# Packed first loads on two queues, a reordered first batch and a reordered end of the last batch in a two-layer MLP with expert output columns

## The reference, cut to what matters

```
h        = gelu(x @ W1 + b1)                    # W1: 512 x 2048
shared   = h @ W2 + b2                          # W2: 2048 x 384
expert_b = h_b @ We[idx_b] + be[idx_b]          # We: 8 x 2048 x 128, one expert for each batch
out      = x + concatenate([shared, expert], -1)
```

## Time and profile before

| what | value |
|---|---|
| median of 3 runs | 1210.66 us (1210.32 to 1212.32) |
| the profiled execution: its own time | 1210.57 us |
| the profiled execution: its span | 1208.8 us |
| TensorE (PE) busy | 1200.3 us, 99% of the span |
| VectorE (DVE) busy | 1063.3 us, 88% |
| ScalarE (ACT) busy | 767.9 us, 64% |
| DMA, mean over the span | 72 GB/s |
| mean granted TensorE clock | 0.999 of full |

### The profile page before, as it was taken

One profiled execution on the slowest core, in us unless ns is written; L12 is line 12 of the kernel. 1 busy time (PEld: TensorE's weight loads), 2 busy tenths in 40 slices (PEclk: granted clock), 3 DMA queues, 4 the chain that ended last, 5 costly groups with the idle time before them and its releaser, 6 DMA issues.

```text
span 1208.8 us, 26221 instructions
## 1 busy us (share of the span) xinstructions
PE 1200.3 (99%) x10284; PEld 1007.5 (83%) x10284; DVE 1063.3 (88%) x1399; ACT 767.9 (64%) x1027; POOL 4.6 (0%) x12
## 2 busy tenths in 40 slices
PE   9999999999999999999999999999999999999998
PEld 4456667778888888888888888888888888888887
DVE  6998888788989988899988989889899888999886
ACT  3765556576766667566765756767666675667652
POOL 0000000000000000000000000000000000000000
PEclk9999999999999999999999999999999999999999
DMA  7316522112131121211212021120311212012101
GB/s 278 105 70 231 198 95 71 36 36 71 36 105 36 35 70 49 91 35 35 71 68 69 35 72 67 35 69 35 104 35 35 69 48 90 35 35 71 70 36 36
DMA packets 38813, 86.61 MB, mean 72 GB/s; under 512 B 5872, under 2 KB 6128, under 8 KB 36208
## 3 DMA queue, kind: packets, MB, share of 16 engines
q1 hardware_dynamic: 37616, 77.63, 19.0%
q0 software_dynamic: 1152, 8.39, 1.9%
HBM read 69.22 MB, written 16.78 MB: 71 GB/s over the span
## 4 chain that ended last, share of the span: by engine, by line
PE 93%; DVE 5%; issue 1%; ACT 1%; DMA 0%; SPq 0%; ACTq 0%; DVEq 0%
PE banks L1635 15%; PE banks L1637 15%; PE banks L1636 15%; PE q_ps L1635 9%; PE q_ps L1637 9%; PE q_ps L1636 9%; PE out_ps L1636 7%; PE out_ps L1635 7%; PE out_ps L1637 7%; DVE h_ring L946 1%; DVE w_max L932 1%; DMA h_ring<-w1f_dram 0%; DVE x_lo L946 0%; ACT u L758 0%; DVE w_lo L946 0%
## 5 line engine op out<-in xcount | busy, mean ns | idle before, releaser
L1635 PE MATMUL banks<-x_hi,w_hi 128*128 128x256 f16 (+1 forms) x1704 | 467.0, 274 | 0.2 <-ACT kept L726 0.2
L1636 PE MATMUL banks<-x_lo,w_hi 128*128 128x256 f16 (+1 forms) x1704 | 467.0, 274 | 0.0
L1637 PE MATMUL banks<-x_hi,w_lo 128*128 128x256 f16 (+1 forms) x1704 | 467.0, 274 | 0.0
L946 DVE SCALAR_TENSOR_TENSOR h_ring<-u,scale,h_ring 128x1536 f16<-128x1536 f32 (+2 forms) x121 | 253.8, 2099 | 24.3 <-ACT h_ring L606 20.4
L726 ACT ACTIVATE kept<-banks 128x512 f32<-128x512 f32 x180 | 106.2, 590 | 173.6 <-PE banks L1637 173.6
L1635 PEld LDWEIGHTS banks<-x_hi,w_hi 128*128 128x128 f16 x1704 | 166.7, 98 | 29.0 <-ACT kept L726 1.0
L1636 PEld LDWEIGHTS banks<-x_lo,w_hi 128*128 128x128 f16 x1704 | 166.7, 98 | 27.2 <-issue 0.3
L1637 PEld LDWEIGHTS banks<-x_hi,w_lo 128*128 128x128 f16 x1704 | 166.7, 98 | 22.0
L758 ACT ACTIVATE u<-u,b_sb,undo 128x512 f32<-128x512 f32 x120 | 91.1, 806 | 101.3 <-DVE u L1254 101.3
L1637 PE MATMUL q_ps<-h_ring,w_lo 128*128 128x256 f16 (+1 forms) x504 | 144.2, 286 | 0.0
L1635 PE MATMUL q_ps<-h_ring,w_hi 128*128 128x256 f16 (+1 forms) x504 | 144.2, 286 | 0.0
(11 more groups left out here) (186 smaller groups left out, 2076.5 us busy)
## 6 DMA issues: line engine op xcount, KB each, us to landing
out_dram<-x_raw SPq DMA_DIRECT2D x63, 256.0 KB, 2.4
x_raw<-x_dram SPq DMA_DIRECT2D x60, 256.0 KB, 4.1
t_sum<-w2o_dram SPq DMA_DIRECT2D x26, 512.0 KB, 3.8
t_sum<-we_dram SPq DMA_DIRECT2D x26, 512.0 KB, 4.3
w_sums<-we_dram POOLq DMA_DIRECT2D x8, 1024.0 KB, 6.5
h_ring<-w_dram SPq DMA_DIRECT2D x5, 1024.0 KB, 8.9
e_raw<-we_dram SPq DMA_DIRECT2D x3, 1024.0 KB, 4.7
t_sum<-w2p_dram SPq DMA_DIRECT2D x2, 1024.0 KB, 4.8
```

Source lines behind the costliest of these rows:

```text
L946: return nc.vector.scalar_tensor_tensor(to, of, s, hi, ALU.mult, ALU.subtract)
L1635: nc.tensor.matmul(ps, hi, v_hi, start=start, stop=False, skip_group_check=True)
L1636: nc.tensor.matmul(ps, hi, v_lo, start=False, stop=False, skip_group_check=True)
L1637: return nc.tensor.matmul(ps, lo, v_hi, start=False, stop=stop, skip_group_check=True)
```

## The change

- The first loads are packed: a new array `first` of two halves, each 128 partitions by 8 KB. Half 0 holds x's input tiles 0 and 1 and W1's (group 0) input tiles 0 and 1, half 1 the rest. Half 0 is loaded by two queues, partitions 0 to 63 by SP and 64 to 127 by ScalarE's (ACT's) queue, half 1 by SP. They land in the ring `h_ring`, no longer in `x_raw`; x of batch 0 is loaded once more into `x_raw[:, 0]` behind W2 of group 2, for the residual. 26 warm-up matmuls become 22.
- TensorE's sum for the scale of x stands behind the fifth matmul of `first_group` instead of behind the third, that for W1's group 1 behind the tenth instead of the ninth, and the other sums of W1, of W2 and of the expert's weights stand later; for batch 0 `e_total` is now behind the sixth unit of layer 2, for batches 1 and 2 behind P2 of step (b, 1).
- VectorE and ScalarE do the work of the first batch in another order. W1's group 1 has its maximum ahead of the lo parts of x; W1's group 2 gets its scale ahead of the maximum of group 0; `w1_split(3)` stands ahead of `h_split(0, 0)`; `w2_split(0)` stands ahead of `e_top(0)`, `w2_split(1)` ahead of `e_scales`, and ScalarE's last two gelus of batch 0 ahead of the expert's splits.
- W2's load of group 3 also waits for the lo parts of x.
- In `TAIL` P1 and P2 of tiles 2 and 3 come ahead of those of tiles 0 and 1, VectorE takes the former first, and the last store of tile 3 is issued by ScalarE.

```
-WARM = 26
+WARM = 22
-TAIL = ((0, P1, 0), (0, P2, 0), (1, P1, 0), (1, P2, 0), (1, P4, 0), (1, P5, 0), (0, P6, 0), (0, P5, 0),
+TAIL = ((1, P1, 0), (1, P2, 0), (0, P1, 0), (0, P2, 0), (1, P4, 0), (1, P5, 0), (0, P6, 0), (0, P5, 0),
...
+        first_raw = h_ring[:, :, :, :, :].rearrange("p r s a n -> p (r s a n)").bitcast(F32)[:, KC * N:3 * KC * N]
+        def first_x_raw(k):
+            return first_raw[:, (k if k < KH else KC + k) * N:][:, :N]
...
-            half = 2 * BLOCK
-            for k in range(2):
-                sp.dma_start(x_raw[:, 0, KH * k:KH * (k + 1)], x[0, :, KH * k:KH * (k + 1)]
-                             ).then_inc(first_x_loaded[k], 16)
-                sp.dma_start(w1_raw(0)[:, half * k:half * (k + 1)], w1f[:, half * k:half * (k + 1)]
-                             ).then_inc(w1_rest_loaded if k else w1_loaded[0], 16)
+            sp.dma_start(first_raw[:P // 2, :KC * N], first[0, :P // 2]).then_inc(first_loaded[0], 16)
+            sp.dma_start(first_raw[:, KC * N:], first[1]).then_inc(first_loaded[1], 16)
...
+            sp.dma_start(x_raw[:, 0], x[0]).then_inc(first_x_again, 16)
+
             sp.wait_ge(w1_max_done, D)
             sp.wait_ge(first_l1_done, C)
+            sp.wait_ge(first_x_lo, KC)
             load_w2(3)
...
-            for o in (1, 2, 3):
+            for o in (1, 2):
                 store(B - 1, 1, o)
...
+            nc.scalar.dma_start(first_raw[P // 2:, :KC * N], first[0, P // 2:]).then_inc(first_loaded[0], 16)
             act.wait_ge(ones_set, 1)
...
             w1_split(2)
-            h_split(0, 0, 0)
             first_gelu(1, 1)
             first_gelu(1, 2)
+            first_gelu(1, 3)
             w1_split(3)
-            first_gelu(1, 3)
+            h_split(0, 0, 0)
             h_split(0, 0, 1)
...
             first_gelu(3, 1)
+            first_gelu(3, 2)
+            first_gelu(3, 3)
             e_split(0, 0)
             e_split(0, 1)
-            first_gelu(3, 2)
-            first_gelu(3, 3)
...
+            act.wait_ge(out_ready[3], B)
+            nc.scalar.dma_start(out[B - 1, 3], x_raw[:, 1, 3]).then_inc(out_stored[3], 16)
...
             first_x_scale()
+            w1_top(1)
             first_x_split(0)
             first_x_split(1)
-            w1_top(1)
             first_x_split(2)
+            w1_scales(1, 3)
             first_x_split(3)
-            w1_scales(1, 3)
+            w1_split(1, 0, 2)
             w1_top(2)
-            w1_split(1, 0, 2)
             w1_split(1, 2, 2)
             w1_top(3)
+            w1_scales(2, 5)
             w1_top(0)
             first_h_top()
-            w1_scales(2, 7)
+            w1_split(2)
             w1_scales(3, 9)
             first_h_scale()
             w1_scales(0, 13)
-            w1_split(2)
+            w1_split(3)
             h_split(0, 0, 0)
-            w1_split(3)
             for d in range(D):
                 w2_top(d)
             h_split(0, 1, 0)
             w2_scales()
+            w2_split(0)
             e_top(0)
-            w2_split(0)
+            w2_split(1)
             e_scales(0, 0)
             e_split(0, 0)
-            w2_split(1)
             e_split(0, 1)
...
-            mix(B - 1, 1, 0)
             take_c11(B - 1, 1)
             take_p1(B - 1, 1, True)
+            mix(B - 1, 1, 0)
             take_xy(B - 1, 1, False)
...
-                        pe.wait_ge(first_x_loaded[k // KH], 16)
-                        pe.wait_ge(w1_loaded[0] if k == 0 else w1_rest_loaded, 16)
+                        pe.wait_ge(first_loaded[k // KH], 16 if k > 0 else 32)
...
-                        if k == 0 and c == 2:
+                        if k == 1 and c == 0:
                             pe.wait_ge(first_x_max_done, KC)
                             total(first_x_tops, first_x_max[:, :]).then_inc(first_x_all_done, 1)
-                        if k == KH and c == 0:
+                        if k == KH and c == 1:
                             w1_total(1)
...
-                    if c == 1:
+                    if c == 0:
+                        w1_total(2)
+                    if c == 3:
 
                         x_total(0)
-                        for d in (2, 3, 0):
+                        for d in (3, 0):
                             w1_total(d)
...
-                    if c == 0:
+                    if c == 1:
                         pe.wait_ge(w2_max_done, D)
...
-                    if c == 2:
-                        e_total(0)
                 for unit in range(OT * C):
                     layer2(0, 0, unit)
+                    if unit == C + 1:
+                        e_total(0)
```

More of the change, by code:

```diff
@@ L86, with build @@
 TOP_SUMS, TOP = 12, 14
-def build(nc, x, idx, w1, w1f, w2, w2p, w2o, we, b1, b2, be, out):
+def build(nc, x, idx, w1, first, w2, w2p, w2o, we, b1, b2, be, out):
     with ExitStack() as ctx:
@@ L166, in build @@
         x_loaded = [sem("x_loaded_even"), sem("x_loaded_odd")]
-        first_x_loaded = [sem(f"first_x_loaded{k}") for k in range(2)]
-        w1_loaded = [sem(f"w1_loaded{d}") for d in range(D)]
-        w1_rest_loaded = sem("w1_rest_loaded")
+        first_loaded = [sem(f"first_loaded{k}") for k in range(2)]
+        first_x_again = sem("first_x_again")
+        w1_loaded = [None] + [sem(f"w1_loaded{d}") for d in range(1, D)]
         w1_reloaded = sem("w1_reloaded")
@@ L266, in place @@
             return h_ring[:, r, part].rearrange("p a n -> p (a n)").bitcast(F32)
+        first_raw = h_ring[:, :, :, :, :].rearrange("p r s a n -> p (r s a n)").bitcast(F32)[:, KC * N:3 * KC * N]
+        def first_x_raw(k):
+            return first_raw[:, (k if k < KH else KC + k) * N:][:, :N]
         def w1_raw(d):
+            if d == 0:
+                return first_raw[:, KH * N:(KH + KC) * N]
             if d == 2:
@@ L273, in w1_raw @@
                 return t_sum[:, :, :, :].rearrange("p a k n -> p (a k n)")
-            return place(d, 1)
+            return place(1, 1)
         s_sum = place(1, 1)
@@ L554, in first_x_split @@
                 act.wait_ge(x_scaled, 1)
-                nc.scalar.activation(first_x[0][:, k], x_raw[:, 0, k], ACT.Copy,
+                nc.scalar.activation(first_x[0][:, k], first_x_raw(k), ACT.Copy,
                                      scale=scale[:, 0, 0:1]).then_inc(first_x_hi, 1)
@@ L701, in residual @@
                 if isinstance(b, int) and b == 0:
-                    act.wait_ge(first_x_lo, KC)
+                    act.wait_ge(first_x_again, 16)
                     act.wait_ge(b2_loaded, 16)
@@ L948, in first_x_top @@
             def first_x_top(k):
-                dve.wait_ge(first_x_loaded[k // KH], 16)
-                top(first_x_max[:, k:k + 1], x_raw[:, 0, k]).then_inc(first_x_max_done, 1)
+                dve.wait_ge(first_loaded[k // KH], 16 if k >= KH else 32)
+                top(first_x_max[:, k:k + 1], first_x_raw(k)).then_inc(first_x_max_done, 1)
             def h_top(b):
@@ L967, in w1_top @@
             def w1_top(d):
-                dve.wait_ge(w1_loaded[d], 16)
                 if d == 0:
-                    dve.wait_ge(w1_rest_loaded, 16)
+                    dve.wait_ge(first_loaded[0], 32)
+                    dve.wait_ge(first_loaded[1], 16)
+                else:
+                    dve.wait_ge(w1_loaded[d], 16)
                 top(w_max[:, d:d + 1], w1_raw(d)).then_inc(w1_max_done, 1)
@@ L1026, in w1_scales @@
             def w1_scales(d, base):
-                dve.wait_ge(w1_all_done, 1 if d == 1 else D)
+                dve.wait_ge(w1_all_done, d if d in (1, 2) else D)
                 power(w1_tops[:, d:d + 1], w_exps[:, :], w1_inv[:, d:d + 1], w1_scale[:, d:d + 1], TOP_SUMS,
@@ L1033, in first_h_top @@
             def first_h_top():
-                base = 5
+                base = 7
                 dve.wait_ge(w1_max_done, D)
@@ L1062, in first_x_split @@
                 dve.wait_ge(first_x_hi, k + 1)
-                split_lo(first_x[1][:, k], x_raw[:, 0, k], scale[:, 0, 0:1], first_x[0][:, k]).then_inc(first_x_lo, 1)
+                split_lo(first_x[1][:, k], first_x_raw(k), scale[:, 0, 0:1], first_x[0][:, k]).then_inc(first_x_lo, 1)
             def add_t(b, par):
@@ L1643, in first_group @@
                     if k % KH == 0:
-                        pe.wait_ge(first_x_loaded[k // KH], 16)
-                        pe.wait_ge(w1_loaded[0] if k == 0 else w1_rest_loaded, 16)
+                        pe.wait_ge(first_loaded[k // KH], 16 if k > 0 else 32)
                     for c in range(C):
-                        last = nc.tensor.matmul(first_bank(c), raw[:, k, c], x_raw[:, 0, k],
+                        last = nc.tensor.matmul(first_bank(c), raw[:, k, c], first_x_raw(k),
                                                 start=k == 0, stop=k == KC - 1)
@@ L1882, in w1_total @@
             def w1_total(d):
-                pe.wait_ge(w1_max_done, 1 if d == 1 else D)
+                pe.wait_ge(w1_max_done, d if d in (1, 2) else D)
```

(11 more changed lines are left out.)

## The result

The changed kernel takes 1214.56 us (median of 7 runs, 1212.93 to 1216.04) against 1210.73 us before (median of 7): ratio 1.0032, 95% interval 1.0022 to 1.0042. It is slower by 3.8 us, where 1210.9 and "no difference" had been forecast. The profiled execution took 1214.53 us, its span is 1212.7 us, 3.9 us longer than before.

A forecast was written before the change was run, and what follows sets the result against it. TensorE, at 99% of the span, was taken to bound the kernel; -1.55 (landing) - 0.3 (short waits) + 2.1 (new waits) + 0 (end) = +0.3 us on 1210.57 gave 1210.9 us, range 1208.8 to 1212.5.

The forecast's parts named there:

- The landing: First packed load: half 0 lands at 5.75 (bounds 5.1 and 7.3), so TensorE starts 1.55 us earlier than 7.30.
- The slow pace of the kernel before: First loads: 248 GB/s in 2 to 4 us before; if it came again, the landing would stay at 7.3.
- The warm-ups: TensorE's start: four fewer warm-ups leave a hole under 0.7 us, the clock stays granted; cost nothing.
- The short waits: TensorE before layer 2: waits for h's scale and for W1's lo part of group 2 both go, -0.3 us.
- VectorE's lateness: First batch up to `x_top` of batch 1 (58.2): VectorE 2.8 us later while TensorE is 1.85 us earlier.
- The three waits: TensorE waits for VectorE near 75, 82 and 96: 1.5, 0.3 and 0.3 us, together +2.1 us (1.5 to 2.7).
- its first 0.3: TensorE's wait at P5 near 82, for `c11` of step (1, 0): 0.3 us.
- its second 0.3: TensorE's wait at P2 of step (1, 1) near 96, for `c12`: 0.3 us.
- The end: Tail: new order and the store moved to ScalarE's queue change nothing, 0 with 0.2 us either way.
- the cushion holds: Rival 1, VectorE's distance to TensorE: the whole head start survives, -1.85 us, 1208.7 us; chance 0.22.
- Rival 2: First load comes no earlier, pace is the bytes', TensorE starts at 7.2: +1.7 us, 1212.3; chance 0.18.
- rival 3: Second load starves ScalarE's part of half 0, TensorE starts at 8.45: +2.95 us, 1213.5; chance 0.08.

The follow-up runs named there:

- a1: Changed kernel with half 0 of the packed load issued whole by SP, 128 partitions, one queue: 1210.83 us, ratio 1.0.
- a3: Changed kernel with half 0 by two queues, each all 128 partitions and half the columns: 1210.74 us, ratio 1.0.
- a4: Changed kernel with 48 warm-up matmuls instead of 22: 1213.35 us, ratio 1.002.
- b2: Kernel before with only the new batch-0 orders of TensorE, VectorE and ScalarE, loads and tail as before: 1212.2 us, ratio 1.0014.
- b3: Kernel before with only the new tail and the last store of tile 3 by ScalarE: 1210.53 us, ratio 0.9998.
- c2: c1 with the tail of the kernel before: 1208.9 us, ratio 0.9985.
- c1: a3 with `e_top(0)` again ahead of `w2_split(0)`, `e_scales` behind it, and TensorE's `e_total(0)` ahead of layer 2: 1208.82 us, ratio 0.9986.
- a2: Changed kernel, but SP issues half 1 only when both parts of half 0 have landed: 1214.59 us, ratio 1.0031.
- b4: Changed kernel with both 64-partition parts of half 0 issued by SP, one behind the other, none by ScalarE: 1215.28 us, ratio 1.004.

## Why the prediction was wrong

**The landing** ("I take 5.75") is the step that failed. The forecast summed over bytes and bounded the pace by 8 KB rows to all 128 partitions, and took the two 64-partition parts for the same thing. For such a transfer the size was right: 5.62 in a1, 5.76 in a3. As the change writes it, half 0 is complete at 8.30, outside the bounds of 5.1 and 7.3. Against the forecast's -1.55 us the start is +1.02 us. No row of the kernel before shows a transfer to half of the partitions, so the bound on the late side should have been wider. Two of its numbers are also off in themselves: 1.8 us off 7.3 is 5.5, not 5.1, and with -0.3 and +2.1 the sum changes its sign at a landing of 5.5, not 5.4. Neither touches the result.

The slow pace of the kernel before, 248 GB/s in 2 to 4 us, is another thing, and here the forecast chose rightly. It lasts until 6 us there, and not in a1 or a3. The window from 4 to 6 us of the kernel before, to be read against the two above:

```profile
4.00:6.00 2.00, 1.80 (x14) 1.29 (x12) 0.62 (x2) 0.00 (x0) 0.00 (x0) 1.00 0.91 236
```

Packing thus does bring the data 1.5 us earlier, as long as all partitions are in each part. Why x and W1 in four separate transfers to 128 partitions each came at 236 GB/s stays open.

The Trainium skill ("DMA: Bandwidth & Descriptors", section "Issuing engines are not separate DMA queues") says that DMAs of several engines share the same 16 engines and only the issue is saved. The runs agree: with 128 partitions one queue lands at 5.62, two at 5.76; with 64, one at 8.02, two at 8.30.

Why 64 partitions halve the pace stays open. The same page, in its section "The descriptor swizzle", shows a transfer to 128 partitions with the engines 0 to 7 writing the partitions 0 to 63 and 8 to 15 the others, each engine one port of the memory. A supposition from it: if all 16 engines serve 64 partitions, two would share each port and the ports of the other 64 stand idle. That fits the full engine share at half the bytes (1.14 and 246 GB/s), and the packets, which are one part's and then the other's, so that both halves of the partitions are not written at once. But no run here counts engines or ports.

**The warm-ups** ("Nothing") failed as a consequence. The forecast leaned on a hole under 0.7 us; it became 2.96 us, the clock was granted at 0.50 in 8 to 10 us, and the float32 group took +1.34 us; the forecast put this term at nothing. a4 confirms it by taking it away. The leaning on the 1.5 us hole was also weaker than it looked: rows 2 and 4 are one execution. Of 75 executions of the kernel before that ran beside the experiments three took 1212.30 to 1212.78 us, at a mean granted clock of 0.998 against 0.999 or 1.000 in the others. The Trainium skill ("TensorE: Matmul & The Clock Gate", Part 1) states that an idle array falls back to its lower clock; these rows agree.

**The short waits** (-0.3) were worth -0.59: 2.36 us late at group 1, 1.77 at layer 2. Bracketed waits were too small a measure. From start to start of the matmuls, where the usual step is 0.22 us, the sums for h and W1 cost 0.49 us before (26.45 to 27.16) and 0.11 us in the changed kernel, and the hole ahead of group 2 cost 0.18 us (32.12 to 32.51) and nothing; the 0.49 us of the earlier trace rows are idle time of the weight loads. In a3 the same step gave -0.60 (from 1.64 to 2.24 us early).

**VectorE's lateness** was right nearly step by step: idle for ScalarE's copy 1.6 forecast, 1.64 measured; lateness against TensorE 2.8 + 1.85 = 4.65 forecast, 4.71 measured; `x_top` of batch 1 at 58.2 forecast, 57.93 in a3. The two parts of the 4.71 were less exact than their sum: in a3 VectorE is 2.48 us later and TensorE 2.24 us earlier. It is a property of the order (4.71 to 4.72 in after, a1, a3, a4 and b2), not of the loads.

**The three waits** (+2.1) measured +2.23: from 1.77 to 4.00 us late. The forecast's 1.5 us stands against 1.57 us lost up to 78.68 (a wait of 1.37 us in the row), its first 0.3 against 0.42 us up to 85.60, and its second 0.3 against 0.21 us up to 100.16, P2 of step (1, 1), which starts right behind the end of VectorE's row of 99.43; 0.03 more are lost up to P6. In a3 they took the head start from 2.24 to 0.

**The end** (0) was right: b3 0.1 us below its before, c2 against c1 nothing.

The sum is then +1.02 + 1.34 - 0.59 + 2.23 = +4.0 us; measured in the profiled executions +3.96. Of the rivals, "the cushion holds" fell: every kernel with the new order shows the waits, until c1 removes their cause. Rival 2 (no earlier landing, by the pace of the bytes) falls with a1 and a3: in the changed kernel the load did come no earlier, at 246 GB/s, near the pace that it named, but the cause is the shape. Its doubt was right that a second queue brings nothing; rival 3 had the right place and nearly the time, but a2 leaves it 0.3 us.

## What to carry to other kernels

Split a load that is waited for by columns, and let each part cover all 128 partitions; a second queue brought nothing, half the partitions cost 2.5 us. Before an engine that never waits is given a head start, count how far ahead of it its suppliers are at every hand-over, and order their lists so that a copy by one engine stands beside work of the other; here 2.24 us of head start were worth 0 until that distance was given back. Warm-up matmuls should reach to the landing that they wait for: in a4 they ran past it and cost 0.57 us at the start, while the holes of 1.96 us (b4) and 2.96 us (the changed kernel) cost 1.58 and 1.34 us more than their own length.

## What of the hardware was not expected

- Parts of 64 partitions ran at 213 to 246 GB/s with a full share of the 16 engines, where the same rows to 128 partitions ran at 414 GB/s (a1), in one queue and in two.
- A hole of 1.5 us between warm-ups and work left the granted clock at full speed in the profiled execution; one of 1.96 us (b4) took it to 0.50 in 10 to 12 us, a loss of 1.58 us, one of 2.96 us to 0.50 in 8 to 10 us and 0.68 in 10 to 12 us, a loss of 1.34 us.
- The changed kernel's runs scatter from 1212.93 us (mean granted clock 1.000) to 1216.04 us (0.996), a1's from 1210.48 to 1211.31. The hole alone doesn't decide it: a2, with one of 2.71 us, stays within 1214.36 to 1214.82, and a4, without one, goes from 1212.73 to 1213.93. The cause stays open.
